# Layer norm of the first batch's rows: sums taken while the rows are made, squares about the mean on ScalarE

## The chip, the cores and the metric

One NeuronCore of a Trainium2 chip runs the kernel. The metric is the device time of one execution in microseconds (us). Engines are named as in the profile: PE is TensorE (PEld its weight loads), DVE is VectorE, ACT is ScalarE, POOL is GpSimd, SP is SyncE, which only issues DMAs here. Each engine works through its own instructions strictly in program order and waits on semaphores.

## The reference, cut to what matters

The layer is a decoder step on x of shape (2, 512, 1024) with a context of (2, 1024, 1024):

```python
x = layernorm(x + attention(x, ...))            # 32 heads, gated, with an RMS scale per row
x = layernorm(x + fake_quant(x) @ fake_quant(ctx))   # 8 bit grid, per batch
x = layernorm(x + ffn(x, up, down, perm))       # columns gathered by perm, 16 heads of 64

def layernorm(x, eps=1e-5):                     # over the 1024 columns of a row
    m, v = mean(x), var(x)
    return (x - m) / sqrt(v + eps)
```

The change is to the first two of these three norms, for the first of the two batches. Each norm needs the mean and the variance of every row.

## The kernel before, in words

Everything is FP32 at the interface. The first 1760 us or so are the attention (projections by split FP16 products on PE); none of that is touched. Behind it comes the **rows phase**, in which rows lie on the 128 partitions. A batch has 512 rows, so four tiles s0 to s3 of 128 rows x 1024 columns; I write b0s0 for tile 0 of batch 0. The tile lives in `acc[b][:, s, :]`. A tile goes through these steps, each a "step" of a plan (`rows_tile`):

1. `row_scale`: a PE product against ones, a small DVE and a small POOL instruction give the row's RMS scale; `load` brings the rows of x into a slot of `raw`.
2. `residual` (DVE, L1460): acc = acc * scale + raw. Then norm 1: `stats` (DVE L1465, L1466, L1468, then POOL L1550 and L1552 for the reciprocal square root), and `normalise` (DVE L1472 makes -mean*rstd, ACT L1271 applies it in place).
3. `quantise`: ACT L1276 scales into a slot of `raw`, DVE L1476 and L1479 clamp and round into a BF16 tile (`q1_n`, named gate_units in the trace).
4. `q1_transpose`: eight PE transposes (L1136), and ACT L1281 copies them to SBUF (`q1_t`, named k_units in the trace).
5. `row_sum` (PE L1144, DVE L1484, L1487) and `ctx_product`: 16 matmuls (L1152) into two PSUM banks, and DVE L1494 adds each of the two halves to acc. Then norm 2, the same instructions as norm 1.
6. `x2_store`: eight PE transposes (L1162), ACT L1288 copies two halves into a slot of `raw`, and ACT issues the DMA to a scratch in HBM (L1292).

The two batches' tiles are interleaved: `rows_phase` is a generator for each batch, and `final_part` steps them in a fixed order (for b0 three steps to one of b1). Each time a generator is stepped it appends plan steps; afterwards every engine's program is written by walking over that one list, so the position of a step in the list is its position on **every** engine that has a part in it. Around the touched norms the list reads (b0 norm steps in capitals): ... STATS b0s2, row_scale b0s3, context_row b0, row_scale b1s0, q1_transpose b0s0, quantise b0s1, normalise b0s2, residual b1s0, stats b1s0, residual b0s3, STATS b0s3, row_sum and ctx_product b0s0, STATS b0s0 (norm 2), q1_transpose b0s1, quantise b0s2, normalise b0s3, normalise b0s0, normalise b1s0, row_sum and ctx_product b0s1, STATS b0s1, q1_transpose b0s2, quantise b0s3, residual and stats b1s1, x2_store b0s0, normalise b0s1, row_sum and ctx_product b0s2, STATS b0s2, row_scale b1s2, q1_transpose b0s3, x2_store b0s1, normalise b0s2, quantise b1s0, row_sum and ctx_product b0s3, STATS b0s3, x2_store b0s2, normalise b0s3, normalise b1s1, x2_store b0s3, residual and stats b1s2, row_scale b1s3, context_row b1, q1_transpose b1s0, and so on with b1 alone, beside the gathers of b0. The feed-forward part follows.

`raw` is a ring of five slots of 128 x 1024 FP32. `Ring.take` gives the next slot that is not held, with the semaphore value at which it is free; the taker's engine waits for that.

Of the kernel before, what the change touches and what calls it, by code (L numbers as in the profile page):

```python
# [4 lines left out]
F32 = mybir.dt.float32  # L5
# [3 lines left out]
ALU = mybir.AluOpType  # L9
ACT = mybir.ActivationFunctionType  # L10

P = 128
B, S, D = 2, 512, 1024
# [30 lines left out]
LAG = 3  # L44
BEHIND = 3
STAGGER = (1, 1)
SCORE_GROUPS = ((0,), (1, 3), (2,))
S_OFF = {0: 0, 1: S, 3: 2 * S - P, 2: 2 * S}
N_SCORES = sum(S - P * j for j in range(ST))
# [2 lines left out]
    ["const_in", "ones_set", "quant_set", "x_hi", "x_lo", "w_hi", "w_lo", "sig", "silu", "qkv_hi", "qkv_lo",  # L52
     "gate_sig", "score_mm", "decayed", "s_hi", "s_lo", "attend_mm", "sq", "gated", "g_hi", "g_lo", "ssq", "out_mm",
     "acc", "ctx_scaled", "ctx_clamped", "row_mm", "row", "norm_mm", "norm_var", "norm_eps", "norm_rstd",
     "resid", "stats", "aggr", "var_eps", "rstd", "shift", "normed", "q1_scaled", "q1_clamped", "q1_n", "q1_tmm",
     "q1_t", "rsum_mm", "rsum", "rowed", "x_mm", "x_acc", "t_mm", "t_copy", "ffn_in", "up_mm", "gelu", "down_mm", "y", "sum_act", "sum1", "sq_pool", "sum2", "sq_last", "total_mm", "mean", "mean2", "var", "var_c",
     "inv", "rs", "y_sub", "y_pool", "y_mul", "stored", "bits_set", "x_t1", "x_t3", "x_t2", "x_t4", "pair_sum",
     "prod_mm", "seeded", "p7_copied", "u3", "c22", "v_mm", "v_copied", "v_sub"]
# [30 lines left out]
class Plan:  # L89
# [292 lines left out]
            self.ring.give(i, self.row_done[b])  # L382
            st["parts"].append(part)

    def norm(self, s, b, ready):
        self.add("stats", b=b, s=s, ready=ready, stats=self.tick("stats"), aggr=self.tick("aggr"),
                 eps=self.tick("var_eps"), rstd=self.tick("rstd"))
        yield None
        st = self.add("normalise", b=b, s=s, rstd=("rstd", self.steps_rstd(b, s)), shift=self.tick("shift"))
        yield self.tick("normed")  # L390

    def steps_rstd(self, b, s):
        return next(st["rstd"][1] for st in reversed(self.steps) if st["kind"] == "stats" and (st["b"], st["s"]) == (b, s))

    def rows_tile(self, b, s):
        i, bank, free = self.ring.take()
        st = self.add("row_scale", b=b, s=s, bank=bank, free=free, ssq=self.ssq_done, mm=self.tick("norm_mm"),
                      var=self.tick("norm_var"))
        rs = self.tick("norm_rstd")
        self.ring.give(i, st["var"])  # L400
        j, landed = self.load(b, s)
        yield
        st = self.add("residual", b=b, s=s, slot=j, rs=rs, landed=landed, acc=self.acc_done[(b, s, 1)])
        done = self.tick("resid")
        self.raw.give(j, done)
        for x1 in self.norm(s, b, done):
            yield

        j, slot, free = self.raw.take()
        st = self.add("quantise", b=b, s=s, slot=slot, free=free, x=x1, scaled=self.tick("q1_scaled"),  # L410
                      clamped=self.tick("q1_clamped"), dst_free=self.q1n_free[(b, s % 2)])
        q1n = self.tick("q1_n")
        self.raw.give(j, q1n)
        yield

        i, bank, free = self.ring.take()
        st = self.add("q1_transpose", b=b, s=s, bank=bank, free=free, q1n=q1n, mm=self.tick("q1_tmm"),
                      dst_free=self.q1t_free[(b, s % 2)])
# [12 lines left out]
        st = self.add("ctx_product", b=b, s=s, rowed=rowed, parts=[])  # L431
        for _ in range(2):
            i, bank, free = self.ring.take()
            part = dict(bank=bank, free=free, mm=self.tick("x_mm"))
            done = self.tick("x_acc")
            self.ring.give(i, done)
            st["parts"].append(part)
        self.q1t_free[(b, s % 2)] = part["mm"]
        for x2 in self.norm(s, b, done):
            yield  # L440

        j, slot, free = self.raw.take()
# [402 lines left out]
class Chip:  # L845


    def __init__(self, nc, stack, dram):
        def sb(name, shape, dt):
            return stack.enter_context(nc.sbuf_tensor(name, shape, dt))  # L850
# [28 lines left out]
        self.small = sb("small", [P, B * ST, 8], F32)  # L879


        self.x2p = [a[:, :, :].rearrange("p t d -> p (t d)").rearrange("p (k s) -> p k s", k=KT) for a in self.acc]
# [98 lines left out]
def until(engine, sem, token):  # L981

    if token is not None:
        engine.wait_ge(sem[token[0]], token[1])
# [211 lines left out]
def scalar_program(act, c, plan):  # L1196
# [4 lines left out]
    for st in plan.steps:  # L1201
# [61 lines left out]
        elif kind == "stash_scale":  # L1263
            src, _ = c.stash_of(st["slot"])
            act.wait_ge(sem[f"pair_in{st['slot']}"], st["landed"][1])
            act.wait_ge(sem["quant_set"], 1)
            act.activation(src, src, ACT.Relu, bias=c.z2, scale=c.inv2).then_inc(sem["ctx_scaled"])
        elif kind == "normalise":
            x, sm = c.acc[b][:, st["s"], :], c.small_of(st)
            act.wait_ge(sem["shift"], st["shift"][1])  # L1270
# [46 lines left out]
def vector_program(dve, c, plan):  # L1317
# [9 lines left out]
    for st in plan.steps:  # L1327
# [127 lines left out]
        elif kind == "residual":  # L1455
# [2 lines left out]
            dve.wait_ge(sem[f"raw_in{st['slot']}"], st["landed"][1])  # L1458
            dve.wait_ge(sem["acc"], st["acc"][1])
            dve.scalar_tensor_tensor(out=x, in0=x, scalar=c.small_of(st)[:, 5:6], in1=c.raw[st["slot"]][:, :],  # L1460
                                     op0=ALU.mult, op1=ALU.add).then_inc(sem["resid"])
        elif kind == "stats":
            x, sm, stats = c.acc[b][:, st["s"], :], c.small_of(st), c.stats_of(st)
            dve.wait_ge(sem[st["ready"][0]], st["ready"][1])
# [3 lines left out]
            dve.bn_aggr(out=sm[:, 0:2], in_=stats[:, :, :]).then_inc(sem["aggr"])  # L1468
        elif kind == "normalise":
            sm = c.small_of(st)  # L1470
            dve.wait_ge(sem["rstd"], st["rstd"][1])
            dve.tensor_scalar(sm[:, 7:8], sm[:, 0:1], sm[:, 3:4], -1.0, ALU.mult, ALU.mult).then_inc(sem["shift"])  # L1472
        elif kind == "quantise":
            src = c.raw[st["slot"]][:, :]
            dve.wait_ge(sem["q1_scaled"], st["scaled"][1])
# [13 lines left out]
        elif kind == "ctx_product":  # L1489
            for half, part in enumerate(st["parts"]):  # L1490
                x = c.acc[b][:, st["s"], half * HALF:(half + 1) * HALF]
                dve.wait_ge(sem["x_mm"], part["mm"][1])
                dve.wait_ge(sem["rowed"], st["rowed"][1])
                dve.scalar_tensor_tensor(out=x, in0=c.banks[part["bank"]][:, :], scalar=c.s12, in1=x, op0=ALU.mult,  # L1494
                                         op1=ALU.add).then_inc(sem["x_acc"])
        elif kind == "down":
            if st["mc"] == 1:
                y = c.x2p[b][:, st["p"], :]
                dve.wait_ge(sem["down_mm"], st["mm"][1])
                dve.tensor_tensor(y, c.banks[st["bank"]][:, :], y, ALU.add).then_inc(sem["y"])  # L1500
        elif kind == "last_stats":
            var, rstd = c.banks[st["banks"][1]][:, :], c.sums[b][1]
            dve.wait_ge(sem["mean2"], st["mean2"][1])
            dve.wait_ge(sem["total_mm"], st["sum2"][1])
            dve.scalar_tensor_tensor(out=var, in0=var, scalar=1.0 / D, in1=rstd, op0=ALU.mult,
                                     op1=ALU.subtract).then_inc(sem["var"])
            dve.wait_ge(sem["var"], st["var"][1])
            dve.tensor_scalar(var, var, 0.0, EPS, ALU.max, ALU.add).then_inc(sem["var_c"])
            dve.wait_ge(sem["var_c"], st["var_c"][1])
            dve.reciprocal(rstd, var).then_inc(sem["inv"])  # L1510
        elif kind == "last_shift":
            if b == 1:
                y = c.x2p[b][:, st["p"], :]
                dve.wait_ge(sem["mean"], st["mean"][1])
                dve.tensor_tensor(y, y, c.sums[b][0], ALU.subtract).then_inc(sem["y_sub"])
        elif kind == "last_scale":
            y = c.x2p[b][:, st["p"], :]
            dve.wait_ge(sem[st["y"][0]], st["y"][1])
            dve.wait_ge(sem["rs"], st["rs"][1])
            dve.tensor_tensor(y, y, c.sums[b][1], ALU.mult).then_inc(sem["y_mul"])  # L1520


def gpsimd_program(pool, c, plan):
    sem, d = c.sem, c.dram
    for st in plan.steps:
# [116 lines left out]
```

## Time and profile before

| what | value |
|---|---|
| median of 3 runs | 1976.84 us (1974.48 to 1980.36) |
| the profiled execution's own time | 1979.36 us |
| its span in the trace | 1976.7 us |
| mean granted TensorE clock | 0.986 of full |
| busy: PE, DVE, ACT, POOL | 1874.7, 1291.2, 866.8, 498.6 us |
| rows phase, from the first `residual` to the last x2_store | 1769.25 to 1868.85 us |

The span is what the trace covers from the first to the last instruction; the time is what the device reports for that execution, 2.7 us more. The shares of the whole span say little here, because PE is busy for 95% of it and the touched stage is 5% of it: the stage has to be read by itself, in the chain of waits and in the timeline.

### The profile page before, as it was taken

What the parts mean: (1) busy time and instruction counts of PE and PEld (TensorE: products, weight loads), DVE (VectorE), ACT (ScalarE), POOL (GpSimd) and SP (SyncE); (2) the same over time, 40 slices, a digit from 0 to 9 for tenths busy, and PEclk for the clock granted to TensorE, in tenths of its full rate; (3) what the DMA queues carried; (4) which work ended last, traced back from release to release, by engine and by line L of the source; (5) the groups of instructions that cost most, each with busy time, mean ns of one, the idle gap of its engine ahead of it and who ended that gap; (6) DMA issues with size and microseconds to landing.
All of it is one profiled execution on the core that took longest, in us unless ns stands there. A gap on an engine that the chain in (4) does not pass through costs nothing.

```text
span 1976.7 us, 25320 instructions
## 1 busy us (share of the span) xinstructions
PE 1874.7 (95%) x9330; PEld 889.1 (45%) x9337; DVE 1291.2 (65%) x1785; ACT 866.8 (44%) x1269; POOL 498.6 (25%) x410
## 2 busy tenths in 40 slices
PE   7999999999999999999999999999999999986895
PEld 4344444444444444444444444444444445543321
DVE  7676776667676767667665757576666666568533
ACT  5453544444343535444443435353444445324552
POOL 2232122221322321222222223222122221013354
PEclk9999999999999999999999999999999999998998
DMA  4112222231312322222222112131212221502311
GB/s 180 46 64 86 65 86 64 93 78 62 102 51 91 80 86 65 87 63 102 70 70 64 48 59 81 54 82 58 58 60 64 75 64 43 202 12 63 110 47 68
DMA packets 105305, 148.52 MB, mean 75 GB/s; under 512 B 62560, under 2 KB 70880, under 8 KB 104160
## 3 DMA queue, kind: packets, MB, share of 16 engines
q1 hardware_dynamic: 93728, 134.23, 21.7%
q0 software_dynamic: 2560, 8.39, 1.3%
q10 hardware_dynamic: 8896, 4.28, 0.7%
q8 instruction: 76, 1.25, 0.3%
q14 instruction: 45, 0.37, 0.1%
HBM read 119.63 MB, written 12.58 MB: 67 GB/s over the span
## 4 chain that ended last, share of the span: by engine, by line
PE 77%; DVE 7%; ACT 5%; DMA 4%; issue 3%; POOL 2%; ACTq 0%; SPq 0%; DVEq 0%; POOLq 0%
PE bank L1036 19%; PE bank L1059 15%; PE bank L1061 15%; PE bank L1060 15%; ACT w_pair L1208 2%; DMA v_split<-w_vo 2%; DVE w_pair L1325 2%; DMA raw_pair<-w_vt 2%; PE bank L1101 2%; PE bank L1103 2%; PE bank L1102 2%; PE bank L1178 2%; PE bank L1170 2%; POOL raw_pair L1534 1%; DVE bank L1380 1%
## 5 line engine op out<-in xcount | busy, mean ns | idle before, releaser
L1059 PE MATMUL bank<-x_blocks,w_pair 128*128 128x512 f16 x1736 | 659.2, 380 | 13.7 <-DVE bank L1368 8.1
L1060 PE MATMUL bank<-x_blocks,w_pair 128*128 128x512 f16 x1736 | 658.7, 379 | 0.0
L1061 PE MATMUL bank<-x_blocks,w_pair 128*128 128x512 f16 x1736 | 658.7, 379 | 0.0
L1036 PE MATMUL bank<-w_vo,gated_split 128*128 128x512 f16 x1440 | 330.6, 379 | 3.8 <-DVE scores_split L1325 3.8
L1533 POOL TENSOR_TENSOR sums_pair<-raw_pair 128x512 f32<-128x512 f32 x62 | 86.9, 1401 | 851.4 <-DVE w_pair L1325 640.0
L1059 PEld LDWEIGHTS bank<-x_blocks,w_pair 128*128 128x128 f16 x1736 | 169.9, 98 | 219.2 <-DVE bank L1368 17.1
L1061 PEld LDWEIGHTS bank<-x_blocks,w_pair 128*128 128x128 f16 x1736 | 170.1, 98 | 205.4 <-issue 1.1
L1060 PEld LDWEIGHTS bank<-x_blocks,w_pair 128*128 128x128 f16 x1736 | 170.1, 98 | 194.0 <-issue 0.8
L1036 PEld LDWEIGHTS bank<-w_vo,gated_split 128*128 128x128 f16 x1440 | 140.9, 98 | 174.0 <-DVE scores_split L1325 5.0
L1325 DVE SCALAR_TENSOR_TENSOR w_pair<-raw_pair,w_pair 128x1024 f16<-128x1024 f32 x124 | 175.5, 1416 | 48.3 <-ACT w_pair L1208 48.3
L1542 POOL TENSOR_TENSOR ssq<-ssq,sig 128x512 f32<-128x512 f32 x64 | 82.7, 1292 | 489.2 <-ACT sig L1259 489.2
L1380 DVE SCALAR_TENSOR_TENSOR bank<-bank,sig 128x512 f32<-128x512 f32 x146 | 101.7, 697 | 144.6 <-ACT sig L1244 142.9
L1391 DVE TENSOR_TENSOR acc<-acc,bank 128x512 f32<-128x512 f32 x240 | 157.7, 681 | 45.1 <-PE bank L1036 43.9
L1253 ACT ACTIVATE scores_split<-bank 128x512 f16<-128x512 f32 (+1 forms) x192 | 101.0, 526 | 120.6 <-DVE bank L1424 116.4
L1244 ACT ACTIVATE sig<-bank 128x512 f32<-128x512 f32 x146 | 86.6, 593 | 122.2 <-PE bank L1061 113.2
L1325 DVE SCALAR_TENSOR_TENSOR w_pair<-sums_pair,w_pair 128x1536 f16<-128x1536 f32 x62 | 108.9, 1756 | 33.1 <-ACT w_pair L1208 32.9
L1244 ACT ACTIVATE sig<-p_copy 128x512 f32<-128x512 f32 x46 | 29.0, 630 | 228.2 <-DVE p_copy L1371 228.2
L1208 ACT ACTIVATE w_pair<-raw_pair 128x1024 f16<-128x1024 f32 x124 | 125.6, 1048 | 0.0
L1325 DVE SCALAR_TENSOR_TENSOR scores_split<-bank,scores_split 128x512 f16<-128x512 f32 (+1 forms) x206 | 118.7, 602 | 9.3 <-ACT scores_split L1247 9.3
L1036 PE MATMUL bank<-q_units,k_units 128*128 128x512 f16 (+3 forms) x768 | 117.4, 304 | 5.9 <-DVE k_units L1325 5.9
L1424 DVE TENSOR_TENSOR bank<-bank,decay_sb 128x512 f32<-128x512 f32 (+3 forms) x256 | 113.7, 490 | 1.9 <-PE bank L1036 1.9
L1228 ACT ACTIVATE p_copy<-bank 128x512 f32<-128x512 f32 x62 | 36.9, 595 | 138.1 <-PE bank L1061 138.0
(172 smaller groups left out, 2190.2 us busy)
## 6 DMA issues: line engine op xcount, KB each, us to landing
raw_pair<-w_qk SPq DMA_DIRECT2D x32, 1024.0 KB, 5.1
raw_pair<-w_gate SPq DMA_DIRECT2D x16, 1024.0 KB, 4.9
raw_pair<-w_out SPq DMA_DIRECT2D x16, 1024.0 KB, 5.2
raw_pair<-w_vt SPq DMA_DIRECT2D x14, 1024.0 KB, 4.9
decay_sb<-decay SPq DMA_DIRECT2D x32, 256.0 KB, 5.2
raw_pair<-ctx_in SPq DMA_DIRECT2D x8, 1024.0 KB, 4.9
acc<-x_t SPq DMA_DIRECT2D x4, 1024.0 KB, 11.8
ctx<-raw_pair SPq DMA_DIRECT2D x8, 512.0 KB, 2.8
```

The lines of the kernel that those rows point to most:

```text
L1036: last = pe.matmul(out, a, b, start=m == 1, stop=m == n)
L1059: pe.matmul(bank[:, :], w_hi, x_hi, start=fresh and k == 0, stop=False, skip_group_check=not fresh)
L1060: pe.matmul(bank[:, :], w_hi, x_lo, start=False, stop=False, skip_group_check=not fresh)
L1061: mm = pe.matmul(bank[:, :], w_lo, x_hi, start=False, stop=k == QT - 1, skip_group_check=not fresh)
L1208: act.activation(hi, src, ACT.Copy, scale=W_SCALE).then_inc(sem["w_hi"])
L1244: act.activation(c.sig32[st["gi"]][:, :], src, ACT.Sigmoid, scale=st["sign"] / W_SCALE).then_inc(sem["sig"])
L1253: act.activation(c.s_hl[:, 0, at:at + width], c.banks[part["bank"]][:, 0:width], ACT.Copy, scale=1.0).then_inc(sem["s_hi"])
L1325: return dve.scalar_tensor_tensor(out=lo, in0=src, scalar=scale, in1=hi, op0=ALU.mult, op1=ALU.subtract)
L1380: dve.scalar_tensor_tensor(out=src, in0=src, scalar=st["sign"] / W_SCALE, in1=c.sig32[st["gi"]][:, :], op0=ALU.mult, op1=ALU.mult).then_in ...
L1391: dve.tensor_tensor(dst, dst, bank[:, :], ALU.add).then_inc(sem["acc"])
L1424: ins = dve.tensor_tensor(ps, ps, c.decay_sb[slot][:, 0:n], ALU.mult)
L1533: pool.tensor_tensor(s3, a11, a21, ALU.add)
```

## The change

For batch 0 (`SUMMED = ((1, 2), ())`: norms 1 and 2 of batch 0, none of batch 1) the `stats` step is replaced by a `squares` step at the same place of the list. The instruction that makes the rows (L1460 for norm 1, L1494 twice for norm 2) also writes out the sum of each row. ACT turns the sum into -mean (one small instruction for norm 1, two for norm 2), then runs Square over all 1024 columns with -mean as bias and writes out the sum of the squares; the squares themselves go into a slot of `raw` and are not used. POOL makes rstd from that, with one instruction more for -mean*rstd, so DVE has no part in `normalise` any more. For norm 1 the slot is the one that held x, given back after the Square and not after the residual. For norm 2 (of both batches) the slot of x2_store is taken where norm 2 begins, two steps of the generator earlier.

```diff
+SUMMED = ((1, 2), ())
@@ norm
-    def norm(self, s, b, ready):
-        self.add("stats", b=b, s=s, ready=ready, stats=self.tick("stats"), aggr=self.tick("aggr"),
-                 eps=self.tick("var_eps"), rstd=self.tick("rstd"))
+    def norm(self, s, b, ready, which, slot, free):
+        if which in SUMMED[b]:
+            means = [self.tick("neg_mean") for _ in range(which)]
+            st = self.add("squares", b=b, s=s, ready=ready, which=which, means=means, slot=slot, free=free,
+                          sum=self.tick("sq_sum"), eps=self.tick("var_eps"), rstd=self.tick("rstd"))
+            shift = self.tick("shift_pool")
+        else:
+            st = self.add("stats", ...)
+            shift = None
+        if which == 1:
+            self.raw.give(slot, st.get("sum", ready))
         yield None
@@ rows_tile, residual
-        self.raw.give(j, done)
-        for x1 in self.norm(s, b, done):
+        for x1 in self.norm(s, b, done, 1, j, None):
@@ rows_tile, behind ctx_product
-        for x2 in self.norm(s, b, done):
+        j, slot, free = self.raw.take()
+        for x2 in self.norm(s, b, done, 2, slot, free):
             yield
-        j, slot, free = self.raw.take()
@@ ACT
+        elif kind == "squares":
+            x, sm, raw = c.acc[b][:, st["s"], :], c.small_of(st), c.raw[st["slot"]]
+            act.wait_ge(sem[st["ready"][0]], st["ready"][1])
+            if st["which"] == 1:
+                act.activation(sm[:, 8:9], sm[:, 0:1], ACT.Copy, scale=-1.0 / D).then_inc(sem["neg_mean"])
+            else:
+                act.activation(sm[:, 8:9], sm[:, 0:1], ACT.Identity, bias=sm[:, 1:2], scale=1.0).then_inc(sem["neg_mean"])
+                act.wait_ge(sem["neg_mean"], st["means"][0][1])
+                act.activation(sm[:, 8:9], sm[:, 8:9], ACT.Copy, scale=-1.0 / D).then_inc(sem["neg_mean"])
+            act.wait_ge(sem["neg_mean"], st["means"][-1][1])
+            until(act, sem, st["free"])
+            act.activation(raw[:, :], x, ACT.Square, bias=sm[:, 8:9], scale=1.0,
+                           accum_out=sm[:, 9:10]).then_inc(sem["sq_sum"])
@@ DVE, residual and ctx_product
+                                     accum_out=c.small_of(st)[:, 0:1] if 1 in SUMMED[b] else None).then_inc(sem["resid"])
+                                         op1=ALU.add, accum_out=c.small_of(st)[:, half:half + 1]
+                                         if 2 in SUMMED[b] else None).then_inc(sem["x_acc"])
@@ POOL
+        elif kind == "squares":
+            sm = c.small_of(st)
+            pool.wait_ge(sem["sq_sum"], st["sum"][1])
+            pool.tensor_scalar(sm[:, 2:3], sm[:, 9:10], 1.0 / D, EPS, ALU.mult, ALU.add).then_inc(sem["var_eps"])
+            pool.wait_ge(sem["var_eps"], st["eps"][1])
+            pool.tensor_tensor(sm[:, 3:4], sm[:, 2:3], c.neg_half[:, 0:1], ALU.pow).then_inc(sem["rstd"])
+            pool.wait_ge(sem["rstd"], st["rstd"][1])
+            pool.tensor_tensor(sm[:, 7:8], sm[:, 8:9], sm[:, 3:4], ALU.mult).then_inc(sem["shift_pool"])
```

## Rows read from the trace of the kernel before

**Rows 1.** Chain of waits, two pieces: start us, us, what.
```profile
1796.03 0.69 DVE stats L1465
...
1828.01 4.33 PE bank L1122 x15
```

**Rows 2.** Busy by stretch: us, PE, PEld, DVE, ACT, POOL (x), PEclk, DMA share, GB/s.
```profile
1797.00:1826.00 29.00, 14.63 (x91) 8.86 (x93) 22.96 (x44) 14.68 (x17) 6.99 (x12) 0.77 0.19 55
1826.00:1834.00 8.00, 6.60 (x36) 3.99 (x36) 2.87 (x6) 3.04 (x5) 2.56 (x5) 0.76 0.43 131
```

**Rows 3.** Groups of DVE instructions: shapes, xcount | busy us, mean ns | idle before.
```profile
L1494 DVE SCALAR_TENSOR_TENSOR acc<-bank,quant_consts,acc 128x512 f32<-128x512 f32 x16 | 11.4, 746 | 0.9
...
L1487 DVE SCALAR_TENSOR_TENSOR acc<-acc,small,q_units 128x1024 f32<-128x1024 f32 x8 | 10.3, 1285 | 0.3
...
L1460 DVE SCALAR_TENSOR_TENSOR acc<-acc,small,raw_pair 128x1024 f32<-128x1024 f32 x7 | 9.0, 1279 | 0.0
...
L1479 DVE TENSOR_SCALAR gate_units<-raw_pair 128x1024 bf16<-128x1024 f32 x6 | 4.2, 693 | 0.2
L1476 DVE TENSOR_SCALAR raw_pair<-raw_pair 128x1024 f32<-128x1024 f32 x6 | 4.1, 682 | 4.3 <-ACT raw_pair L1276 4.3
...
L1472 DVE TENSOR_SCALAR small<-small 128x1 f32<-128x1 f32 x16 | 3.1, 206 | 4.7 <-POOL small L1552 4.7
```

**Rows 4.** Groups of ACT instructions, same columns.
```profile
L1208 ACT ACTIVATE w_pair<-raw_pair 128x1024 f16<-128x1024 f32 x124 | 125.6, 1048 | 0.0
...
L1253 ACT ACTIVATE scores_split<-bank 128x256 f16<-128x256 f32 x64 | 24.6, 384 | 27.7 <-DVE bank L1424 27.7
...
L1271 ACT ACTIVATE acc<-acc,small 128x1024 f32<-128x1024 f32 x16 | 19.4, 1237 | 42.4 <-DVE small L1472 42.4
```

**Rows 5.** Groups of POOL instructions, same columns.
```profile
L1552 POOL TENSOR_TENSOR small<-small,neg_half 128x1 f32<-128x1 f32 x16 | 12.9, 804 | 1.3
...
L1550 POOL TENSOR_SCALAR small<-small 128x1 f32<-128x1 f32 x16 | 5.3, 329 | 59.7 <-DVE small L1468 59.7
```

**Rows 6.** Timeline, 1780 to 1800: start us, us, engine line, what [idle before].
```profile
1783.80 1.02 ACT L1281 ACTIVATE k_units<-bank 128x1024 bf16<-128x1024 bf16 x1 [1.49 <-PE bank L1136]
...
1785.13 3.61 PE L1152 MATMUL bank<-x_blocks,k_units 128*128 128x512 bf16 x16
...
1789.22 1.02 ACT L1281 ACTIVATE k_units<-bank 128x1024 bf16<-128x1024 bf16 x1 [0.42 <-PE bank L1136]
...
1790.14 1.23 ACT L1276 ACTIVATE raw_pair<-acc,quant_sb,quant_consts 128x1024 f32<-128x1024 f32 x1
...
1791.55 0.69 DVE L1465 BATCH_NORM_STATS2 stats<-acc 128x6 f32<-128x512 f32 x1
...
1792.99 0.16 DVE L1484 TENSOR_SCALAR small<-bank,quant_consts 128x1 f32<-128x1 f32 x1
...
1794.58 1.41 DVE L1494 SCALAR_TENSOR_TENSOR acc<-bank,quant_consts,acc 128x512 f32<-128x512 f32 x2
...
1797.49 0.68 DVE L1476 TENSOR_SCALAR raw_pair<-raw_pair 128x1024 f32<-128x1024 f32 x1
...
1799.07 3.51 ACT L1271 ACTIVATE acc<-acc,small 128x1024 f32<-128x1024 f32 x3 [7.69 <-DVE small L1472]
```

**Rows 7.** Timeline, 1804 to 1826.
```profile
1804.51 1.06 ACT L1288 ACTIVATE raw_pair<-bank 128x512 f32<-128x512 f32 x2
...
1805.60 0.39 ACTq L1292 DMA_DIRECT2D x_t<-raw_pair  x1
...
1820.07 1.41 DVE L1494 SCALAR_TENSOR_TENSOR acc<-bank,quant_consts,acc 128x512 f32<-128x512 f32 x2
...
1824.29 2.37 ACT L1271 ACTIVATE acc<-acc,small 128x1024 f32<-128x1024 f32 x2 [6.26 <-DVE small L1472]
...
1825.58 1.97 PE L1162 MATMUL bank<-ident,acc 128*128 128x128 f32 x8 [8.51 <-ACT acc L1271]
```

**Rows 8.** DMA issues, 1765 to 1870: line, xcount, KB each, median us to landing.
```profile
x_t<-raw_pair ACTq DMA_DIRECT2D x7, 512.0 KB, 3.2
```

More of the change, by code:

```diff
@@ L54 @@
      "acc", "ctx_scaled", "ctx_clamped", "row_mm", "row", "norm_mm", "norm_var", "norm_eps", "norm_rstd",
-     "resid", "stats", "aggr", "var_eps", "rstd", "shift", "normed", "q1_scaled", "q1_clamped", "q1_n", "q1_tmm",
+     "resid", "stats", "aggr", "neg_mean", "sq_sum", "var_eps", "rstd", "shift", "shift_pool", "normed", "q1_scaled", "q1_clamped", "q1_n", "q1_tmm",
      "q1_t", "rsum_mm", "rsum", "rowed", "x_mm", "x_acc", "t_mm", "t_copy", "ffn_in", "up_mm", "gelu", "down_mm", "y", "sum_act", "sum1", "sq_pool", "sum2", "sq_last", "total_mm", "mean", "mean2", "var", "var_c",
@@ L383, in context_row @@
             st["parts"].append(part)
-    def norm(self, s, b, ready):
-        self.add("stats", b=b, s=s, ready=ready, stats=self.tick("stats"), aggr=self.tick("aggr"),
-                 eps=self.tick("var_eps"), rstd=self.tick("rstd"))
+    def norm(self, s, b, ready, which, slot, free):
[5 more added lines that the diff above has]
+        else:
+            st = self.add("stats", b=b, s=s, ready=ready, stats=self.tick("stats"), aggr=self.tick("aggr"),
+                          eps=self.tick("var_eps"), rstd=self.tick("rstd"))
+            shift = None
+        if which == 1:
+            self.raw.give(slot, st.get("sum", ready))
         yield None
-        st = self.add("normalise", b=b, s=s, rstd=("rstd", self.steps_rstd(b, s)), shift=self.tick("shift"))
+        st = self.add("normalise", b=b, s=s, rstd=st["rstd"], shift=shift or self.tick("shift"), own=shift is None)
         yield self.tick("normed")
-    def steps_rstd(self, b, s):
-        return next(st["rstd"][1] for st in reversed(self.steps) if st["kind"] == "stats" and (st["b"], st["s"]) == (b, s))
     def rows_tile(self, b, s):
@@ L878, in __init__ @@
         self.stats = sb("stats", [P, B * ST, 2, 6], F32)
-        self.small = sb("small", [P, B * ST, 8], F32)
+        self.small = sb("small", [P, B * ST, 10], F32)
         self.x2p = [a[:, :, :].rearrange("p t d -> p (t d)").rearrange("p (k s) -> p k s", k=KT) for a in self.acc]
@@ L1267, in scalar_program @@
             act.activation(src, src, ACT.Relu, bias=c.z2, scale=c.inv2).then_inc(sem["ctx_scaled"])
+        elif kind == "squares":
[11 more added lines that the diff above has]
+                           accum_out=sm[:, 9:10]).then_inc(sem["sq_sum"])
         elif kind == "normalise":
             x, sm = c.acc[b][:, st["s"], :], c.small_of(st)
-            act.wait_ge(sem["shift"], st["shift"][1])
+            until(act, sem, st["shift"])
             act.activation(x, x, ACT.Identity, bias=sm[:, 7:8], scale=sm[:, 3:4]).then_inc(sem["normed"])
@@ L1460, in vector_program @@
             dve.scalar_tensor_tensor(out=x, in0=x, scalar=c.small_of(st)[:, 5:6], in1=c.raw[st["slot"]][:, :],
-                                     op0=ALU.mult, op1=ALU.add).then_inc(sem["resid"])
+                                     op0=ALU.mult, op1=ALU.add,
+                                     accum_out=c.small_of(st)[:, 0:1] if 1 in SUMMED[b] else None).then_inc(sem["resid"])
         elif kind == "stats":
@@ L1470, in vector_program @@
             sm = c.small_of(st)
-            dve.wait_ge(sem["rstd"], st["rstd"][1])
-            dve.tensor_scalar(sm[:, 7:8], sm[:, 0:1], sm[:, 3:4], -1.0, ALU.mult, ALU.mult).then_inc(sem["shift"])
+            if st["own"]:
+                dve.wait_ge(sem["rstd"], st["rstd"][1])
+                dve.tensor_scalar(sm[:, 7:8], sm[:, 0:1], sm[:, 3:4], -1.0, ALU.mult, ALU.mult).then_inc(sem["shift"])
         elif kind == "quantise":
@@ L1494, in vector_program @@
                 dve.scalar_tensor_tensor(out=x, in0=c.banks[part["bank"]][:, :], scalar=c.s12, in1=x, op0=ALU.mult,
-                                         op1=ALU.add).then_inc(sem["x_acc"])
+                                         op1=ALU.add, accum_out=c.small_of(st)[:, half:half + 1]
+                                         if 2 in SUMMED[b] else None).then_inc(sem["x_acc"])
         elif kind == "down":
```

## The prediction

> **What bounds the kernel now.** I started with the page: PE is busy 95% of the span, which says nothing of the 100 us in which rows are normalised. So the chain of waits came next, cut to that stretch. From 1785 to 1825 it runs through DVE nearly without a break, the statistics passes among its pieces, and at 1828 it goes over to PE's context row of batch 1 [rows 1]. The reader is to see two things: the statistics do lie on the path, and everything of batch 1 behind 1828 is queued on PE behind the x2_store transposes of b0s3. The busy times by stretch, read third, say how tight it is: in 1797 to 1826 DVE works 23.0 of 29 us and ACT 14.7, and in 1826 to 1834 DVE and ACT have 3 us each of 8 [rows 2]. So whatever time b0s3's second normalise gains or loses, the end gains or loses, as far as nothing behind it was waiting for something else. The timeline, read last, shows what ACT does in its idle time: it copied b0s1's transposes at 1789.22 and scaled b0s2 for quantising at 1790.14, and then stood idle 7.69 us [rows 6]. DVE took that scaled tile at 1797.49 with no wait [rows 6]: ACT had run ahead of it.
>
> **What goes, and its price.** Statistics of one norm: 0.69 us for a half, another for the other, and an aggregate; from the start of b0s3's first (1791.55) to the next instruction (1792.99) it is 1.44 us [rows 6]. With them goes DVE's shift, 0.21 us [rows 3], and the waits for POOL in front of it. Five such norms (b0s3's first and the four second ones) lie between 1791 and 1823: 5 * 1.65 = 8.3 us of DVE. The three earlier ones (b0s0 to b0s2, first) lie mostly beside the last out matmuls on PE.
>
> **What comes, and its price.** On ACT the Square over 1024 columns with a per-partition bias: L1271 has that shape and costs 1.24 us [rows 4]. The small instructions have no row on ACT. Bounds: 384 ns for 256 columns and 1048 for 1024 leave 0.16 at no columns; 1.05 us without and 1.24 with per-partition operands say 0.19 more for those [rows 4]. I take 0.22 for the copy and 0.40 for the add with a bias, and 0.03 for each hand-over. The accumulator outputs have no row either. Both ends: nothing, or one more small instruction. On DVE such a one is 0.21 at most (L1472); I take 0.15, nearer to that row, since a sum has to be written somewhere. On ACT I take 0.20 and keep 0 to 0.40. The Trainium skill, page "VectorE: DVE Perf Modes", section "Two Vector instructions with no wait between them", says that an op which writes out its accumulator is two instructions; by the lower bound the sum below would be 2.5 us smaller, and no row of this trace shows which holds. POOL gets a third instruction, between 0.33 and 0.80 by its other two [rows 5]; I take 0.35. For b0s3's last norm it ends while ACT still copies b0s2's x2, so it costs nothing; without that cover it would be the 0.35.
>
> So a squares step of norm 2 holds ACT for 0.03 + 0.40 + 0.03 + 0.22 + 0.03 + 1.24 + 0.20 = 2.15 us, one of norm 1 for 1.75.
>
> **What it moves: ACT's place in the queue.** The step sits where the statistics sat, and there ACT had nothing. Now ACT must wait there for DVE. Behind squares b0s0 (norm 2) are queued the copy of b0s1's transposes and the scaling of b0s2; before they ran at 1789.22 and 1790.14, now not before b0s0's adds end and the Square is through. PE's row sum and context product of b0s1 wait for the copy, and DVE's clamp of b0s2 waits for the scaling. DVE's next row work waits for both. So ACT and DVE take turns instead of working side by side, and the DVE time saved is spent in waiting. Turn by turn, from the end of a tile's adds to that of the next (DVE pieces: clamp and round 0.68 + 0.69 + 0.05; L1487 with its two small ones 1.64; adds 1.41 + 2 * 0.15 = 1.71 [rows 3, 6]; ACT pieces: copy 1.02, scaling 1.23 [rows 6]):
> - b0s0 to b0s1: ACT 2.15 + 1.02 + 1.23 = 4.4; DVE 1.42 + shift of b1s0 0.2 + 1.64 + 1.71 = 5.0. 9.4 us.
> - b0s1 to b0s2: ACT 4.4; DVE 1.42 + residual 1.30 and statistics 1.44 of b1s1 + 1.64 + 1.71 = 7.5. 11.9 us.
> - b0s2 to b0s3: on ACT the x2 copies of b0s1 1.06, the DMA issue 0.39 with its wait 0.06 [rows 7], normalise b0s2 1.24 [rows 4] and the scaling of b1s0 stand behind the copy: 2.15 + 1.02 + 1.06 + 0.45 + 1.24 + 1.23 = 7.15; DVE 1.42 + 1.64 + 1.71 = 4.8. 12.0 us.
>
> That is 33.3 us where before it is from 1795.99 to 1821.48, 25.5 us [rows 6, 7]: +7.8.
>
> **The start.** Squares b0s1 stands in front of the scaling of b0s0, squares b0s2 in front of the copy of b0s0's transposes (before: 1783.80 [rows 6]). The first holds DVE's clamps back, so that b0s2's residual ends near 1783.5; the second then ends at 1783.5 + 1.75 = 1785.25, and the copy is 1.5 us late. Against that, b0s3's first statistics no longer stand on DVE before b0s0's adds (-1.44), and three accumulator writes do (+0.45): b0s0's adds end 0.5 us later.
>
> **The tail.** Before, the second normalise of b0s3 ended 4.05 us behind the last add (1821.48 to 1825.53 [rows 7]). Now ACT runs 2.15 of squares, x2 copies of b0s2 1.06, a DMA issue 0.45, the normalise 1.24, with 0.15 of hand-overs: 5.05. +1.0. Then PE's transposes (1.97 [rows 7]) and the context row (4.33 [rows 1]) follow as before, and with them batch 1.
>
> **Sum**: 7.8 + 0.5 + 1.0 = +9.3 us. With no price for accumulators (-2.5) and the smallest one for small instructions (-0.7) it is +6.1; with 0.21 and 0.40 for the accumulators (+1.6) and the clock of the second rival (+1.8) it is +12.7.
>
> **Other edits.** The slots of raw change. For norm 2 of b0s2 the Square writes into the slot out of which b0s0's x2 is still being stored, and for b0s3 into that of b0s1: DMAs take 3.2 us to land [rows 8]; by my times the first is issued near 1811.6 and the Square wants the slot near 1818.6, the second 1822.3 and 1830. Both hidden by 3 us or more; without that cover the wait would be up to 3.2 each. SP's load for b1s2 now waits for the residual of b1s1; it is needed 15 us later. Nothing is added to any DMA queue. Batch 1 keeps its statistics.
>
> **How the time is formed.** The profiled execution took 1979.36 us for a span of 1976.7, 2.7 outside. Its span becomes 1986.0, its time 1988.7. It lies 2.5 above the median of the three runs; against the median, 1976.84 + 9.3 = 1986.1.
>
> **Rivals.**
> - *The relief is kept (faster).* DVE sets the chain from 1785 to 1825 [rows 1]; its 8.3 us less 9 accumulator writes at 0.15 and 1 us of ACT would give -6: 1971. The skill's page "Perfetto Trace Analysis", section "Optimizing Scalar/DVE Operations", argues this way: with DVE saturated, moving work to Scalar may make sense. It decides by whether the copy and the scaling reach ACT before DVE asks: they would have to be done by 1797. Their place in the list is behind squares of b0s0, whose input is DVE's add at 1794.58 [rows 6], so at best 1800. 0.08.
> - *The clock makes it worse.* The granted clock is already 0.77 in 1797 to 1826 with PE busy half of it [rows 2]; in the new order PE stands still 8 us before b0s1's context product. The 16 matmuls took 3.6 us at 2.4 GHz [rows 6]; at 1.2 GHz throughout they take near 7 (estimate: twice the spacing), and the second half comes 1.8 us after DVE wants it. With dear accumulators: +13, 1989.8. 0.10.
> - *Batch 1 takes part of the delay up.* Its residual and statistics of s2 will be done before b0s3's x2 copies, so DVE meets the tail of the phase with less to do; for a gain some wait behind 1834 must be DVE's own. No row before 1834 says how much of it is; both its residuals with statistics, 2 * 2.7 = 5.5 us, and a shift are what could fall out, 6 of 9 us: +3, 1979.8. 0.18.
> - *It doesn't do what it says*: were the slots' waits or an accumulator to serialise further, it goes with the second rival's price.
>
> **Chances.** Forecast 0.64, clock 0.10, part taken up 0.18, relief 0.08. The measurement can tell about 0.3%, 5.9 us, from no change. Slower by more: forecast and clock, 0.74. Within: 0.18. Faster: 0.08. The range takes in the rival with +3 and both ends of the sum with 1.5 us for the runs' spread: 1979.5 to 1991.0; only the relief lies outside, and what my working misses.
>
> **What would show it.** In the profile after: no L1465 before b1's first; DVE idle before its clamps, released by ACT's scaling, 2 to 3.5 us for each of b0s2, b0s3 and b1s0; the ACT copies of b0s1 to b0s3 right behind a Square, some 9.5, 5.5 and 11 us later than before; squares steps of 2.15 us; the last x2 transposes of b0 at 1834.9 where they were at 1825.58 [rows 7]; the same distance from there to the end. Wrong it would be if the copy and the scaling were found ahead of the Square, or if the distance from b0's last x2 transposes to the end shrank.

## The result and the profile after

The changed kernel takes 1980.78 us (median of 10 runs, 1980.04 to 1982.71), the one before, run beside it, 1976.41 (10 runs). The ratio is 1.0022, 95% interval 1.0014 to 1.0030: **4.3 us slower, 2.8 to 5.9**. That is the forecast's direction and a little under half of its size (+9.3). It is also less than the 5.9 us that I had called the least that the measurement can tell, a case to which I had given 0.18. With ten runs of each the interval still keeps clear of zero.

The two spans, 1977.8 and 1976.7, seem to say that it costs 1 us. They mislead, for the first thing that differs lies ahead of the rows phase. This is TensorE's time by stretch, the last out matmuls of the attention in it; the columns are as in [rows 2]. Before:

```profile
1766.00:1771.00 5.00, 5.00 (x13) 1.84 (x12) 2.32 (x3) 0.00 (x0) 0.49 (x1) 0.50 0.00 0
```

After:

```profile
1764.00:1769.00 5.00, 5.00 (x25) 2.48 (x26) 3.25 (x6) 1.44 (x3) 0.59 (x2) 1.00 0.00 0
```

In the profiled run of before the clock was at its lower level there (granted 0.50, 13 matmul records in 5 us), in that of after at the upper (25 in 5 us). The same code took other values between these in other kernels below. A stage has therefore to be measured by itself. I measure from the first matmul of b0's context row to the first of b1's, both on PE: before 1779.78 to 1828.01 [rows 1], **48.2 us**. After, in the timeline:

```profile
1774.99 3.40 PE L1130 MATMUL bank<-x_blocks,ones 128*128 128x512 bf16 x15
...
1788.92 0.75 DVE L1517 SCALAR_TENSOR_TENSOR acc<-bank,quant_consts,acc 128x512 f32<-128x512 f32 x1
...
1789.60 0.74 DVE L1517 SCALAR_TENSOR_TENSOR acc<-bank,quant_consts,acc 128x512 f32<-128x512 f32 x1
...
1826.10 1.97 PE L1170 MATMUL bank<-ident,acc 128*128 128x128 f32 x8 [6.30 <-ACT acc L1292]
...
1828.53 4.67 PE L1130 MATMUL bank<-x_blocks,ones 128*128 128x512 bf16 x15 [0.24 <-issue]
```

**53.5 us**: 5.3 us more. The two anchors don't shut the clock out altogether. The first piece of the stage, up to the end of b0s0's adds, takes 16.2 us in before but 16.8 in slots_only and sums_only (table below), which have the same work there and whose out matmuls ahead of it ran faster. The last piece, from b0s3's x2 transposes to b1's context row, takes 1.4 to 2.4 us, by the clock that the transposes and what follows them are granted. So a difference of two stages is good to some 0.6 us in the first piece and 1 us in the last. Against slots_only (48.4) the changed kernel loses 5.1 us.

L1517 is the add of a tile's halves (L1494 before), L1170 b0s3's x2 transposes. The waits of DVE between 1775 and 1826 say where the loss is (who waited for whom: us in total, times, longest). Before:

```profile
DVE raw_pair L1476 <- ACT raw_pair L1276: 2.4, 1, 2.4
DVE small L1472 <- POOL small L1552: 2.3, 3, 1.0
...
DVE sums_pair L1476 <- ACT sums_pair L1276: 0.4, 1, 0.4
```

After:

```profile
DVE sums_pair L1499 <- ACT sums_pair L1297: 10.3, 2, 6.5
DVE raw_pair L1499 <- ACT raw_pair L1297: 7.3, 3, 3.9
DVE acc L1517 <- PE bank L1160: 0.7, 1, 0.7
```

DVE's clamps (L1499) now wait 17.6 us for ACT's scaling (L1297) where they waited 2.8. One turn in the timeline, from b0s0's adds to the clamp of b0s2, shows why:

```profile
1790.39 0.29 ACT L1282 ACTIVATE small<-small 128x1 f32<-128x1 f32 x1 [1.51 <-DVE acc L1517]
1790.71 0.20 ACT L1284 ACTIVATE small<-small 128x1 f32<-128x1 f32 x1
1790.95 1.15 ACT L1287 ACTIVATE raw_pair<-acc,small 128x1024 f32<-128x1024 f32 x1
1792.00 0.19 ACT L1287 ACTIVATION_READ_ACCUMULATOR raw_pair<-acc,small 128x1 f32 x1
1792.10 1.00 ACT L1302 ACTIVATE k_units<-bank 128x1024 bf16<-128x1024 bf16 x1
...
1793.00 1.23 ACT L1297 ACTIVATE sums_pair<-acc,quant_sb,quant_consts 128x1024 f32<-128x1024 f32 x1
...
1793.20 0.35 PE L1152 MATMUL bank<-ones,k_units 128*128 128x1 bf16 x8 [7.83 <-issue]
...
1794.26 0.69 DVE L1499 TENSOR_SCALAR sums_pair<-sums_pair 128x1024 f32<-128x1024 f32 x1 [3.84 <-ACT sums_pair L1297]
```

The copy (L1302) and the scaling stand behind the Square (L1287). Before, both had started by 1790.14, 4.4 us ahead of the adds at 1794.58 [rows 6]; now DVE stands idle 3.84 us and PE 7.83 us.

The stage in pieces, in us. Start: first context row to the end of b0s0's adds. Turns: end of a tile's adds to the end of the next tile's. Tail: end of b0s3's adds to its x2 transposes; 2.0 to 2.4 us follow to b1's context row, 1.4 in short_square. Each line is one profile. Time is the ratio against before, in us, with its 95% interval; after_2, short_square_2 and the other kernels are explained below.

| kernel | start | turn 1 | turn 2 | turn 3 | tail | stage | time against before |
|---|---|---|---|---|---|---|---|
| before | 16.2 | 6.7 | 9.2 | 9.6 | 4.1 | 48.2 | |
| after | 15.4 | 9.2 | 11.0 | 11.0 | 4.55 | 53.5 | +4.3 (2.8 to 5.9) |
| after_2 | 15.4 | 9.3 | 11.0 | 11.0 | 4.55 | 53.7 | +4.2 (2.4 to 5.9) |
| slots_only | 16.8 | 6.7 | 9.2 | 9.6 | 4.1 | 48.4 | +0.6 (-1.2 to 2.4) |
| sums_only | 16.8 | 6.7 | 9.2 | 9.6 | 4.1 | 48.8 | +0.4 (-1.6 to 2.2) |
| norm1_only | 15.5 | 6.7 | 8.6 | 9.6 | 4.1 | 46.5 | -2.0 (-3.8 to -0.2) |
| norm2_only | 16.9 | 9.8 | 11.0 | 11.0 | 4.55 | 55.3 | +6.5 (4.2 to 8.9) |
| norm2_s0 | 16.7 | 9.8 | 9.1 | 9.6 | 4.1 | 51.7 | +2.8 (1.0 to 4.7) |
| short_square | 14.6 | 8.8 | 10.2 | 10.1 | 3.7 | 48.8 | +2.8 (1.0 to 4.5) |
| short_square_2 | 14.6 | 9.1 | 10.2 | 10.1 | 3.7 | 50.1 | +1.8 (0 to 3.4) |
| pe_kept_busy | 15.3 | 8.4 | 11.0 | 11.0 | 4.55 | 52.4 | +4.9 (3.2 to 6.9) |
| squares_later | 15.6 | 5.8 | 10.1 | 12.2 | 4.5 | 50.2 | +0.6 (-1.2 to 2.4) |
| own_place | 15.6 | 5.6 | 10.3 | 10.1 | 4.6 | 48.2 | -0.4 (-2.2 to 1.4) |
| norm1_both | 13.8 | 6.5 | 7.2 | 11.0 | 4.1 | 45.0 | -6.9 (-9.7 to -4.2) |

### The profile page after: what moved, and what is told of

The parts are those of the page before. It is cut to its first block, busy times and chain, and to the rows that moved or that the text cites. A ratio compares the mean times of both kernels' runs of the same rounds, so it can differ in the third digit from the quotient of the medians.

```text
span 1977.8 us, 25340 instructions
## 1 busy us (share of the span) xinstructions
PE 1872.6 (95%) x9330; PEld 887.5 (45%) x9337; DVE 1278.2 (65%) x1765; ACT 878.7 (44%) x1297; POOL 497.5 (25%) x418
## 4 chain that ended last, share of the span: by engine, by line
PE 78%; DVE 7%; ACT 5%; DMA 4%; issue 4%; POOL 2%; ACTq 0%; SPq 0%; DVEq 0%; POOLq 0%
PE bank L1044 19%; PE bank L1067 15%; PE bank L1069 15%; PE bank L1068 15%; ACT w_pair L1216 2%; DMA raw_pair<-w_vt 2%; PE bank L1109 2%; DVE w_pair L1346 2%; DMA v_split<-w_vo 2%; PE bank L1111 2%; PE bank L1110 2%; PE bank L1186 2%; PE bank L1178 2%; POOL raw_pair L1558 1%; PE bank L1160 1%
```

## The experiments

**The two norms apart.** The tuple that names the norms is all that changes.

```diff
-SUMMED = ((1, 2), ())
+SUMMED = ((), ())      # slots_only
+SUMMED = ((1,), ())    # norm1_only
+SUMMED = ((2,), ())    # norm2_only
```

> The new order of the raw slots alone, statistics on DVE for all norms. All theories: no difference from before (0 +- 1 us), since no slot was waited for. The profile also answers a second question: in the profile of before twelve out matmuls ahead of the rows phase took 5.28 us (half clock), in that of the changed kernel 2.75 us. If that is chance, this kernel can show either; if it shows the short one and its median is still that of before, chance it is. A rival by which the slot order costs the 4.4 us would see +4 here.

> Squares only for norm 1 of batch 0. Queue theory (the loss comes from norm 2, where ACT has to wait for DVE's adds with the next tile's copy and scaling queued behind): the start part of the changed kernel alone, b0s0's last add 0.9 us earlier after the context row than before, turns between tiles as before (6.7, 9.2, 9.6 us): -1 us. Rival 'work' (each Square put on ACT costs the same wherever it stands): half of the loss, +2 us.

> Squares only for norm 2 of batch 0. Queue theory: the whole loss and a little more, since the start's gain is missing: turns 9.2, 11.0, 11.0 us as in the changed kernel against 6.7, 9.2, 9.6 before, +5.5 us in all. Rival 'work': half of the loss, +2 us. Together with norm1_only it must add up to the changed kernel's +4.4.

The order in which slots are taken costs nothing: +0.6 us, interval through zero, all turns as before. (The later giving back in norm 1 isn't in this kernel; it is in norm1_only, which is faster than before.) Its profile has the out matmuls at a value in between (4.2 us for the twelve), so that part of the profile is chance. Norm 1 alone is 2.0 us *faster* than before and norm 2 alone 6.5 slower; together +4.5, the changed kernel's +4.3. "Each Square costs the same" falls: four of them gain, four lose. The queue theory had -1 and +5.5. Both lie in the intervals, but the stage says that it undervalued both: norm 1 gains 0.6 in turn 2 as well, and norm 2 has 9.8 us in turn 1 and not 9.2, with 1.15 us of DVE waiting for PE in it.

**One tile.** norm2_s0 has squares only for norm 2 of b0s0.

```diff
-SUMMED = ((1, 2), ())
+SUMMED = ((2,), ())
+SUMMED_TILES = (0,)
...
-        if which in SUMMED[b]:
+        if which in SUMMED[b] and s in SUMMED_TILES:
...
```

> Squares only for norm 2 of b0s0, statistics on DVE everywhere else. Queue theory: the turn from b0s0's adds to b0s1's goes from 6.7 to some 9.2 to 10 us, since the copy and the scaling stand behind the Square; the later turns are as before (9.2, 9.6): +2.5 to 3.3 us against before. Rival 'work': one eighth of the loss, +0.6. Rival 'some later step makes up for it': 0.

+2.8 us, and in the trace turn 1 alone is longer (9.8 for 6.7); the two later turns are as before. The loss is local to the turn in which the Square stands in front of the copy, and nothing behind makes it up.

**The place in ACT's queue.** squares_later keeps every instruction and its size, and changes only where ACT comes to three of them.

```diff
+def scalar_steps(plan):
+    steps = list(plan.steps)
+    for s, behind in ((0, "quantise"), (1, "quantise"), (2, "q1_transpose")):
+        i = next(i for i, st in enumerate(steps) if st["kind"] == "squares" and (st["s"], st["which"]) == (s, 2))
+        st = steps.pop(i)
+        j = next(j for j in range(i, len(steps)) if steps[j]["kind"] == behind)
+        steps.insert(j + 1, st)
+    return steps
...
-    for st in plan.steps:
+    for st in scalar_steps(plan):
```

> The changed kernel with every instruction and its size kept; only on ACT the squares of norm 2 of b0s0 and b0s1 move behind the scaling of the next tile, that of b0s2 behind the copy of the next tile's transposes. Queue theory: turns of about 5.2, 10.3, 10.3 us, 25.8 in all instead of 31.2, so 5 us faster than the changed kernel and within 1.5 us of before. Rival 'work' or 'longer norm' (the chain through ACT and POOL is what costs): the same time as the changed kernel, +4.4, or more, since squares come even later. Rival 'accumulators': likewise +4.4.

3.7 us faster than the changed kernel (+0.6 against +4.3, intervals apart): the place costs. It isn't the chain from the adds through ACT and POOL to the normalise, which for b0s1 is longer here (6.6 us for 5.3). In the timeline of squares_later the copy starts just before b0s0's adds and the scaling runs during them, and DVE waits 0.53 us and not 3.84:

```profile
1790.56 1.00 ACT L1313 ACTIVATE k_units<-bank 128x1024 bf16<-128x1024 bf16 x1
...
1791.38 0.74 DVE L1528 SCALAR_TENSOR_TENSOR acc<-bank,quant_consts,acc 128x512 f32<-128x512 f32 x1
1791.47 1.23 ACT L1308 ACTIVATE sums_pair<-acc,quant_sb,quant_consts 128x1024 f32<-128x1024 f32 x1
...
1792.73 0.69 DVE L1510 TENSOR_SCALAR sums_pair<-sums_pair 128x1024 f32<-128x1024 f32 x1 [0.53 <-ACT sums_pair L1308]
```

But turn 3 took 12.2 us for the expected 10.3. The cause is one line of the same timeline, a wait for a store out of the slot into which the Square writes:

```profile
1810.68 1.15 ACT L1298 ACTIVATE raw_pair<-acc,small 128x1024 f32<-128x1024 f32 x1 [2.11 <-DMA x_t<-raw_pair]
```

This is the wait that the prediction had called hidden as long as the Square comes late. own_place takes it away, by another place for the unused squares.

```diff
-            until(act, sem, st["free"])
+            if st["which"] == 2:
+                raw = c.squares_out
...
+        self.squares_out = v_flat[:, 0:4 * S].bitcast(F32)
```

> squares_later with one edit: the Squares of norm 2 write their unused output into 1024 columns that the attention left free, not into the slot of raw. In squares_later the Square of b0s2 waits 2.1 us for the store of b0s0's x2 out of that slot, and the scaling of b1s0 stands behind it. Queue theory: that wait goes, turn 3 is 10.1 instead of 12.2 us, the stage between the context rows 48.1 instead of 50.2 us, that is as before (48.2): 2 us faster than squares_later, within 1.5 us of before. Rival 'longer norm' (the normalise comes later through ACT and POOL, whatever is freed): the stage stays at 50 us or so and turn 3 over 11.

Turn 3 is 10.1 and the stage 48.2: as expected, to 0.1 us. The time is that of before; the expected 2 us against squares_later can't be seen in it (-0.4 against +0.6, intervals overlapping). So with three Squares later, the changed kernel gains and loses nothing against before. But its norm 1 alone would have gained: against norm1_only (stage 46.5) the Squares of norm 2 still cost 1.7 us (turn 1 is 1.0 shorter, turn 2 is 1.6 longer, turn 3 and the tail 0.5 each). Why shows in DVE's waits for ACT's scaling in own_place, in turn 2 and in turn 3:

```profile
1799.67 0.69 DVE L1512 TENSOR_SCALAR raw_pair<-raw_pair 128x1024 f32<-128x1024 f32 x1 [3.15 <-ACT raw_pair L1310]
...
1812.46 0.69 DVE L1512 TENSOR_SCALAR sums_pair<-sums_pair 128x1024 f32<-128x1024 f32 x1 [5.60 <-ACT sums_pair L1310]
```

ACT has become the one that is waited for: between b0s2's adds and the second of these scalings (b1s0's) it does two small ones, a Square, two x2 copies, a DMA issue and a normalise. In norm1_only the first wait isn't there and the second is 2.4 us. The second scaling still stands behind a Square; a kernel in which b0s2's Square comes behind it too was not run.

**The work of the Square.** short_square keeps place and waits and takes the work away.

```diff
-            act.activation(raw[:, :], x, ACT.Square,
+            act.activation(raw[:, 0:8], x[:, 0:8], ACT.Square,
```

> The changed kernel with the Square of every squares step cut to 8 of 1024 columns: every wait, order and small instruction stays, about 0.95 us of ACT work goes from each of the eight steps. The variance then comes from 8 columns (that part of the computation is changed). Queue theory, by which ACT and DVE take turns, so that all of a squares step is on the path: three turns and the tail lose 0.95 each and the start some 0.9, together 4.7 us faster than the changed kernel, and about as fast as before (+-1 us). Rival 'only the place costs': ACT waits for the adds in any case, so the size hardly matters and it stays at +3 to +4.4 against before. Rival 'hidden work': the same.

> The changed kernel once more, unedited, beside the next one, because the two were timed on different occasions and the gap between them (4.4 against 2.8 us over before) is smaller than their profiles say (stage between the two context rows 53.5 against 48.8 us). All theories: about +4.4 us against before. In its profile the stage takes 53.5 us within 1, and what varies is outside of it.

> The Square over 8 of 1024 columns once more (the variance comes from 8 columns), unedited. Queue theory with all of the step on the path: 4.7 us faster than the changed kernel run beside it, stage 48.8 us. If the earlier +2.8 against before was real, something outside the stage gives 2 us back, and the gap is 1.5 us again.

The Square's row goes from 1.15 to 0.30 us. Start, turns 2 and 3 and tail lose 0.8 to 0.9 each in both profiles, so there the step's length is on the path in full; "only the place costs" falls. Turn 1 loses only 0.2 to 0.45, since DVE, come earlier, waits longer for PE (1.44 us in short_square_2 for the 0.68 in the changed kernel). That makes 3.5 us, and 3.5 is what the stage shrinks by in short_square_2 against after_2. In the first profile it is 4.8, but 1.0 of that is the clock: short_square's last x2 transposes took 1.09 us for eight and the context row followed 1.45 us behind their start, where after, after_2 and short_square_2 have 1.97 and 2.4. Over that piece the granted clock was 0.89 in short_square and 0.50 in short_square_2. So the expected 4.7 was 1.2 too much, 0.75 of it in turn 1. The times agree with the smaller figure: short_square_2 and after_2, run beside each other, have medians 3.1 us apart (1978.79 and 1981.85); the earlier pair, from different occasions, gives 1.5 by the ratios.

**The clock.** pe_kept_busy runs 28 matmuls in PE's gap before b0s1's row sum.

```diff
+            if b == 0 and st["s"] == 1:
+                pe.wait_ge(sem[f"ctx_in{b}"], st["ctx"][1])
+                for k in range(28):
+                    pe.matmul(bank[:, :], c.ones16[:, :], c.ctx_q[b][k % KT][:, 0:HALF], start=True, stop=True)
```

> The changed kernel with 28 matmuls more on PE (results overwritten), in the gap in which it waits for the copy of b0s1's transposes. Rival 'clock': in the changed kernel that product starts at 1.2 GHz and DVE waits 0.7 us for its second half. With PE at 2.4 GHz that wait goes: turn 1 is 8.5 instead of 9.2 us, 0.7 us in all. If the clock were a main cause of the loss, 2 us or more. Queue theory: no more than the 0.7.

In the timeline of after_2 b0s1's context product behind a gap:

```profile
1795.10 0.35 PE L1152 MATMUL bank<-ones,k_units 128*128 128x1 bf16 x8 [7.83 <-issue]
1795.70 5.08 PE L1160 MATMUL bank<-x_blocks,k_units 128*128 128x512 bf16 x15 [0.24 <-issue]
```

and in pe_kept_busy, PE busy until 1.7 us ahead of it:

```profile
1794.89 0.35 PE L1156 MATMUL bank<-ones,k_units 128*128 128x1 bf16 x8 [1.72 <-ACT k_units L1306]
1795.10 3.61 PE L1164 MATMUL bank<-x_blocks,k_units 128*128 128x512 bf16 x15
```

3.6 us for 5.1: the granted clock is 1.00 over this product, so it ran at 2.4 GHz throughout, where after_2 has 0.50 (1.2 GHz) until 1797.3. DVE's wait for the second half is gone, and turn 1 is 8.4 for 9.3. The clock's part of the loss is these 0.9 us, of one turn. In the time it can't be seen (+4.9 against +4.2, intervals overlapping).

**The accumulators.** sums_only is the kernel before with the accumulator outputs and nothing that uses them.

```diff
-                                     op0=ALU.mult, op1=ALU.add).then_inc(sem["resid"])
+                                     op0=ALU.mult, op1=ALU.add,
+                                     accum_out=c.small_of(st)[:, 8:9] if b == 0 else None).then_inc(sem["resid"])
...
-                                         op1=ALU.add).then_inc(sem["x_acc"])
+                                         op1=ALU.add, accum_out=c.small_of(st)[:, 8 + half:9 + half]
+                                         if b == 0 else None).then_inc(sem["x_acc"])
```

> The kernel before with nothing changed but the accumulator outputs of batch 0's twelve row-making DVE instructions, whose sums nobody uses. By the profile of the changed kernel a read of DVE's accumulator is a row of 0.08 us that overlaps its neighbours: no difference from before (0 +- 1 us), and add-to-add distance 0.67 us as before. As priced in the prediction, 0.15 each with nine on the path: +1.35 us, distance 0.81.

Its timeline:

```profile
1792.03 0.75 DVE L1495 SCALAR_TENSOR_TENSOR acc<-bank,quant_consts,acc 128x512 f32<-128x512 f32 x1
1792.71 0.08 DVE L1495 DVE_READ_ACCUMULATOR acc<-bank,quant_consts,acc 128x1 f32 x1
1792.71 0.75 DVE L1495 SCALAR_TENSOR_TENSOR acc<-bank,quant_consts,acc 128x512 f32<-128x512 f32 x1
```

From add to add it is 0.68 us. Without the output two adds of 0.75 us took 1.41 together [rows 6], so their starts were 0.66 apart. The read has a row of its own and takes no time on DVE.

**A version that beats both.** Norm 1 is where the exchange pays, so norm1_both makes it for both batches.

```diff
-SUMMED = ((1, 2), ())
+SUMMED = ((1,), (1,))
```

> Squares for norm 1 of both batches, statistics for norm 2 of both. In norm 1 ACT waits for a residual of DVE that ends early, with little queued behind. Queue theory: besides the 1.7 to 2 us of norm 1 of batch 0, the statistics of b1s0 and b1s1 leave DVE's chain, 1.6 us each, while ACT has idle time there: 4 to 5 us faster than before. Rival: squares of b1s1 stand on ACT in front of the x2 copies and the normalise of b0 and hold these up by 1 to 2 us: then only 2 us faster than before, as with batch 0 alone, or less.

6.9 us faster than before (4.2 to 9.7), 1969.39 us in the median, and 11 below the changed kernel's median of another occasion. In the stage it is 3.2 us: b1s0's statistics went from DVE's chain in the start and b1s1's in turn 2 (7.2 for 9.2). Turn 3 lost 1.4 of that, as the rival had it. In turn 2 the Square of b1s1 waits for its residual (2.69 us) with b0s0's x2 copies (L1309) behind it; b0s1's normalise and x2 copies come later for it, and in turn 3 DVE waits 3.80 us for the scaling of b1s0 behind them, where it waited 2.44 before. Part of this is the clock again: b0s1's x2 transposes took 1.92 us here (granted clock 0.53 over 1804.77 to 1806.50) and 1.09 before.

```profile
1800.56 0.20 ACT L1280 ACTIVATE small<-small 128x1 f32<-128x1 f32 x1 [2.69 <-DVE acc L1481]
...
1800.80 1.15 ACT L1287 ACTIVATE raw_pair<-acc,small 128x1024 f32<-128x1024 f32 x1
...
1801.94 1.06 ACT L1309 ACTIVATE raw_pair<-bank 128x512 f32<-128x512 f32 x2
...
1810.18 0.69 DVE L1499 TENSOR_SCALAR sums_pair<-sums_pair 128x1024 f32<-128x1024 f32 x1 [3.80 <-ACT sums_pair L1297]
```

Behind the stage, from b1's context row to the end of b1s0's adds, it takes 12.3 us where before took 14.2 (1828.01 to 1842.21), and the turn to b1s2's adds is 7.3 for 7.9. To the start of b1s3's x2 transposes that makes 36.1 us for before's 38.6; the other kernels, with batch 1's statistics on DVE, have 38.9 to 40.0. So 5.6 of the 6.9 us lie in these two parts. The remainder is within what the rest varies by: from b1s3's x2 transposes to the end of the span it is 109.5 us here, 110.1 in before and 112.9 in slots_only, for the same code.

## Why the prediction was right in its mechanism and wrong in its size

- **That ACT's place in the queue decides: right.** squares_later and norm2_s0 show it. The waits that the prediction named (DVE before its clamps, released by ACT's scaling) are 3.84, 3.91 and 6.51 us; it had 2 to 3.5, too low by its own turns, in which ACT holds DVE for 4.4, 4.4 and 7.15.
- **The failing step is the sum's prices.** Stage by stage: start +0.5 forecast, -0.9 measured (15.4 for 16.2; -1.4 against slots_only); turns 33.3 forecast, 31.2 measured, against 25.5 before; tail +1.0 forecast, +0.45 measured. Sum +9.3 forecast, +5.3 in the trace, +4.3 in the time. Of the 4.0 too much in the trace the accumulators are 2.5 and durations taken for distances some 2.2; a wait that the sum lacked takes 0.7 off. The next three points show them.
- *Accumulators.* I took 0.15 on DVE and 0.20 on ACT "since a sum has to be written somewhere", together 2.5 us. On DVE they cost nothing (sums_only). On ACT the Square and its read take 1.15 us to the next instruction, as long as L1271 of the same shape and without one (three of them took 3.51 [rows 6]). The Trainium skill's rule, page "VectorE: DVE Perf Modes", section "Two Vector instructions with no wait between them", that an accumulator output makes two instructions is confirmed by the rows: the read has its own, of 0.08 us. It costs no time, so the lower bound of nothing was the right value.
- *Durations added where starts count.* The squares step of norm 2, from the end of the adds to the next ACT instruction, was forecast 2.15 (0.20 of it the accumulator's) and measured 1.76 (1790.34 to 1792.10); the copy 1.02 and measured 0.90 from its start to the next; a normalise 1.24 for 1.14. Consecutive rows overlap by 0.1 us on ACT. For DVE's statistics I had taken the distance of starts (1.44), for ACT the durations, on four to seven pieces a turn. The small instructions measured 0.20 and 0.29, for 0.22 and 0.40. The 2.2 us for these together are what remains of the 4.0; no run shows them by themselves.
- *Against these*, in the other direction, turn 1 holds 0.68 us that the sum did not have: DVE's wait for the product's second half. It stood only in the clock rival, which had 1.8; pe_kept_busy gives 0.9.
- **That the time fell inside the stated range is no merit of the sum.** With prices at their lowest it was still +6.1; the range reached down to 1979.5 only because it took in the rival "batch 1 takes a part up", which didn't happen.
- **The start had the wrong sign.** ACT's copy of b0s0's transposes came 0.8 us late and not 1.5 (1779.83 against 1783.80 [rows 6], each from its context row), and the three accumulator writes cost nothing; what is left is that b0s3's statistics (1.44 us) are gone.
- **The reading of the chain was too simple.** From 1785 to 1825 it doesn't run through DVE nearly without a break. The chain's own view has it on ACT from 1799.07 to 1804.64, 5.6 us, and on POOL and ACT from 1813.53 to 1817.09, 3.6 us. b0s1's second statistics (1802.69) run beside ACT's copy and scaling and weren't on the chain, so less than 8.3 us was there to be saved, and ACT's work was partly on it before anything moved there.

```profile
1799.07 0.69 ACT acc L1271
...
1801.35 1.23 ACT acc L1271
...
1803.38 1.23 ACT sums_pair L1276
1804.64 0.72 DVE sums_pair L1476
...
1815.83 1.24 ACT raw_pair L1276
1817.09 0.70 DVE raw_pair L1476
```

- **Norm 1 and norm 2 were priced as one change.** Apart, by the stage, norm 1 is -1.7 and norm 2 +7.1 (against slots_only -1.9 and +6.9). The prediction's own argument (how long ACT waits at that place, and what stands behind it) would have separated them.
- **Relief kept** (0.08): didn't happen, for the reason given. Its promise of -6 wasn't reached with three Squares later either: own_place gives 0, because ACT then sets turns 2 and 3. The rule that moving work from a saturated DVE to Scalar may make sense (the Trainium skill's page "Perfetto Trace Analysis", section "Optimizing Scalar/DVE Operations") holds in norm1_both (-6.9 us) and not in norm 2 (+6.5 us).
- **Batch 1 takes a part up** (0.18): the time, +4.3, lies near its +3, but not by its mechanism. From b0s3's x2 transposes to the end of the span it is 151.7 us after and 151.1 before (1976.7 less 1825.58 [rows 7]): nothing was given back there.
- **Clock** (0.10): part of it came true. PE stood still 7.83 us before b0s1's product, which then took some 5 us and not near 7, and it cost 0.9 us and not 1.8.
- **Slots and POOL: right.** No Square of the changed kernel waited for its slot, POOL's third instruction took 0.19 us, and slots_only is as before.

## What to carry to other kernels

Work that is moved to an idle engine must be looked at by its place in that engine's queue: what stands behind it there, and how long the engine will wait for the new input. Where the input comes early (norm 1) the exchange gained 2 to 7 us, where it comes last (norm 2) it lost 6.5, with the same Square and only one small instruction more. Price each place apart, and add distances between starts and not durations.

## What the runs showed of the hardware

- Accumulator outputs are free in time here: on DVE a row of 0.08 us in the shadow of the next start, on ACT 0.19 us within the Square's 1.15. The Square over 8 columns with the same operands has a row of 0.30 us.
- The clock that TensorE is granted in one and the same piece of code differs between profiles: twelve matmuls took 5.28 us in before, 4.17 in slots_only and 2.75 in after. These 2.5 us are more than half of the effect, so two single spans can't show it. The distance between two points around the changed stage repeated within 0.2 us for the changed kernel (53.5, 53.7), but only within 1.3 for short_square (48.8, 50.1), 1.0 of it from the clock of the last eight transposes. Pieces of the stage between two instructions of DVE repeated best, within 0.1 us but for turn 1.
